# A Gram stage in a recommendation tower: one 108x108 float32 product for four neighbouring items in place of four 27x27 strip products

## What is computed

```python
e = jnp.stack([tbl_0[ids[:, 0]], ..., tbl_25[ids[:, 25]]], axis=1)      # 2048 x 26 x 128
combined = jnp.concatenate([e, r_dense_x[:, None, :]], axis=1)          # 2048 x 27 x 128
interact = jnp.einsum('bfd,bgd->bfg', combined, combined)
z = interact[:, _TRIU_I, _TRIU_J]                                       # 351 pairs
h = jnp.concatenate([z, r_dense_x], axis=1)
h = jnp.maximum(h @ W_top1 + b_top1, 0.0)                               # 479 -> 512
h = jnp.maximum(h @ W_top2 + b_top2, 0.0)                               # 512 -> 256
y = h @ W_top3
```

## Time and profile before

| | before |
|---|---|
| median of 3 runs | 605.26 us (597.03 to 606.22) |
| the profiled execution | 600.04 us, its span 598.2 us |
| mean granted TensorE clock | 0.778 of full speed |
| PE busy | 367.6 us (61% of the span) |
| PE weight loads busy | 335.5 us (56%) |
| POOL busy | 300.0 us (50%) |
| ACT busy | 180.2 us (30%) |
| DVE busy | 176.4 us (29%) |
| mean DMA rate | 81 GB/s |

### The profile page before, as it was taken

One profiled execution on the slowest core, in us unless ns is written; L12 is line 12 of the kernel. 1 busy time (PEld: TensorE's weight loads), 2 busy tenths in 40 slices (PEclk: granted clock), 3 DMA queues, 4 the chain that ended last, 5 costly groups with the idle time before them and its releaser, 6 DMA issues.

```text
span 598.2 us, 13682 instructions
## 1 busy us (share of the span) xinstructions
PE 367.6 (61%) x6108; PEld 335.5 (56%) x6108; DVE 176.4 (29%) x390; ACT 180.2 (30%) x257; POOL 300.0 (50%) x295
## 2 busy tenths in 40 slices
PE   0130836858386846867584847774685568467847
PEld 0130836848285736766483847674575467356846
DVE  3112932625031521343132411352034313102100
ACT  1140411414143332315050412334151425034401
POOL 6774584637455473636376654737373737500000
PEclk9965866869588876958596877979597779659865
DMA  5981521436131462144124423144221413111010
GB/s 114 217 222 46 113 54 46 118 72 137 36 98 45 118 90 84 49 83 115 60 71 76 106 70 90 48 104 100 73 61 46 127 35 94 41 57 59 3 57 0
DMA packets 46250, 48.40 MB, mean 81 GB/s; under 512 B 18504, under 2 KB 38801, under 8 KB 46192
## 3 DMA queue, kind: packets, MB, share of 16 engines
q1 hardware_dynamic: 36544, 28.63, 21.3%
q0 software_dynamic: 9216, 18.89, 11.7%
q10 hardware_dynamic: 432, 0.00, 0.0%
HBM read 37.01 MB, written 10.49 MB: 79 GB/s over the span
## 4 chain that ended last, share of the span: by engine, by line
PE 54%; issue 31%; ACT 4%; DVE 3%; another core or an unknown queue 3%; DMA 3%; SPq 1%; ACTq 0%; DVEq 0%
PE ps_o L559 21%; PE ps_g L587 13%; PE ps_l L611 9%; PE ps_l L622 5%; PE ps_t L574 5%; ACT emb L337 1%; PE ps_l L631 1%; DMA emb<-tbl 1%; ACT emb L330 1%; DVE tab L437 1%; DMA turn<-gram 1%; DMA zl<-turn 1%; ACT h L355 1%; DVE onehot L449 1%
## 5 line engine op out<-in xcount | busy, mean ns | idle before, releaser
L214 POOL DMA_INDIRECT rows<-tbl,idx x288 | 299.2, 1039 | 218.0 <-PE ps_t L574 137.2
L559 PE MATMUL ps_o<-onehot,tab 128*128 128x256 f32 (+1 forms) x1024 | 141.8, 299 | 31.4 <-DVE tab L437 19.4
L559 PEld LDWEIGHTS ps_o<-onehot,tab 128*128 128x128 f32 (+1 forms) x1024 | 134.9, 205 | 35.9 <-DVE tab L437 19.7
L587 PE MATMUL ps_g<-emb 128*27 128x27 f32 x4096 | 79.8, 220 | 119.0 <-issue 116.5
L449 DVE TENSOR_SCALAR onehot<-ids_b,row_of 128x512 fp32r<-128x512 int32 (+1 forms) x256 | 113.1, 495 | 92.4 <-PE ps_o L559 58.4
L587 PEld LDWEIGHTS ps_g<-emb 128*27 128x27 f32 x4096 | 63.0, 133 | 136.2 <-issue 131.6
L337 ACT COPY emb<-ps_t 128x512 f32<-128x512 f32 (+1 forms) x80 | 89.9, 1185 | 136.8 <-PE ps_t L574 136.8
L574 PE MATMUL ps_t<-ident,rows 128*128 128x128 f32 x304 | 53.6, 313 | 54.0 <-issue 39.6
L330 ACT COPY emb<-ps_o 128x512 f32<-128x512 f32 x32 | 38.2, 1193 | 131.5 <-remote 65.0
L574 PEld LDWEIGHTS ps_t<-ident,rows 128*128 128x128 f32 x304 | 39.2, 159 | 58.0 <-issue 40.9
L611 PE MATMUL ps_l<-zh,w_sb 117*128 117x256 f32 (+1 forms) x216 | 48.8, 348 | 8.6 <-DVE zl L469 8.6
(11 more groups left out here) (26 smaller groups left out, 143.7 us busy)
## 6 DMA issues: line engine op xcount, KB each, us to landing
ids_b<-ids_oh SPq DMA_DIRECT2D x32, 256.0 KB
turn<-gram SPq DMA_DIRECT2D x16, 432.0 KB
rows<-tbl,idx POOLq DMA_INDIRECT x288
turn<-gram SPq DMA_DIRECT2D x16, 208.0 KB
zl<-turn SPq DMA_DIRECT2D x64, 40.5 KB
emb<-tbl SPq DMA_DIRECT2D x8, 256.0 KB
emb<-tbl SPq DMA_DIRECT2D x8, 192.0 KB
rows<-r_dense_x SPq DMA_DIRECT2D x16, 64.0 KB
```

The costliest lines, as they stand in the source:

```text
L214: nc.gpsimd.indirect_dma_start(out=rows[u][:, v, :], out_offset=None, in_=gathered[GATHERED.index(SLOT_OF[v])], in_offset=bass.IndirectOff ...
L559: last = nc.tensor.matmul(ps_o[n % 2][:, j, :], tab[0:r, UNIT * o + j, part, k, :], onehot[m % BUFS][0:r, i, j, :], start=(k, j, part) == ...
L587: last = nc.tensor.matmul(ps_g[h][SLOT * s:SLOT * s + NF, NF * g:NF * (g + 1)], v, v, start=True, stop=True)
```

## The change

Four neighbouring items, whose 108 columns lie side by side in `emb`, are multiplied with themselves in one 108x108 product; the four 27x27 blocks on its diagonal are the wanted matrices, the other twelve are not used. A bank now holds four such products, so a tile fills eight banks in turn (`GBANKS`) instead of two, in the same two PSUM banks. The even ones are copied by DVE, the odd ones by ACT, each 108 rows by 432 elements, to the one `gram` buffer left, and PE waits before each bank for the copy of the bank two before. Both copies wait for the stores of the tile before. `spread` stores only the diagonal blocks: 27 rows at a time, two DMAs for each of the four, eight in all. The order of items inside a tile becomes s + 4g, so the copies of x and of y read or write with a stride. The zeroing of the banks goes. One-hot buffers become four of one block each, instead of three of two blocks. The `keep_gram` in the diff is ACT's; DVE has the same over `range(0, GBANKS, 2)`.

```diff
-KB = 2
+KB = 1
-BUFS = 3
+BUFS = 4
-S4, SLOT = 4, 32
+S4, SM = 4, 4
 GROUPS = TILE // S4
-HALF = GROUPS // 2
+BANKG = 4
+GBANKS = GROUPS // BANKG
+GCOLS = SM * NF
+TURN_DMAS = 2 * S4
-        gram = [sb(f"gram{u}", [P, NF, GROUPS]) for u in range(2)]
+        gram = sb("gram", [P, SM, NF, GROUPS])
+        def strip_at(s):
+            return NF * s, s % SM
+        def gram_of(h):
+            return gram[0:GCOLS].rearrange("p s j g -> p (s j) g")[:, :, BANKG * h:BANKG * (h + 1)]
+        def products_of(h):
+            return ps_g[h % 2][0:GCOLS, 0:BANKG * GCOLS].rearrange("p (g c) -> p c g", c=GCOLS)
...
             def spread(tile):
                 u = tile % 2
-                sp.wait_ge(gram_moved, 2 * tile + 2)
+                for h in range(2):
+                    sp.wait_ge(gram_kept[h], GBANKS // 2 * (tile + 1))
                 if tile >= 2:
                     sp.wait_ge(z_in[u], Z_DMAS * 16 * (tile // 2))
-                to = turn[u].ap()
-                flat = gram[u][:].rearrange("p j g -> p (j g)")
-                sp.dma_start(to[:, 0:NF * GROUPS], flat).then_inc(turn_out[u], 16)
-                sp.dma_start(to[:, NF * GROUPS:], flat[:, 0:LAST_D * GROUPS]).then_inc(turn_out[u], 16)
+                to = turn[u].ap().rearrange("(s i) n -> s i n", s=S4)
+                for s in range(S4):
+                    p, c = strip_at(s)
+                    own = gram[p:p + NF, c].rearrange("p j g -> p (j g)")
+                    sp.dma_start(to[s, :, 0:NF * GROUPS], own).then_inc(turn_out[u], 16)
+                    sp.dma_start(to[s, :, NF * GROUPS:], own[:, 0:LAST_D * GROUPS]).then_inc(turn_out[u], 16)
...
+            def keep_gram(tile):
+                if tile:
+                    act.wait_ge(turn_out[(tile - 1) % 2], TURN_DMAS * 16 * ((tile + 1) // 2))
+                for h in range(1, GBANKS, 2):
+                    act.wait_ge(gram_done, GBANKS * tile + h + 1)
+                    nc.scalar.copy(gram_of(h), products_of(h)).then_inc(gram_kept[h % 2], 1)
...
-                for h in range(2):
-                    if tile:
-                        pe.wait_ge(gram_moved, 2 * tile + h - 1)
-                    for g in range(HALF):
-                        for s in range(S4):
-                            v = item_of(t % 2, cols + GROUPS * s + HALF * h + g)
-                            last = nc.tensor.matmul(ps_g[h][SLOT * s:SLOT * s + NF, NF * g:NF * (g + 1)], v, v,
-                                                    start=True, stop=True)
+                for h in range(GBANKS):
+                    if tile or h >= 2:
+                        pe.wait_ge(gram_kept[h % 2], (GBANKS * tile + h) // 2)
+                    for g in range(BANKG):
+                        b = cols + S4 * (BANKG * h + g)
+                        v = emb[t % 2][:, b:b + SM, :].rearrange("p b f -> p (b f)")
+                        last = nc.tensor.matmul(ps_g[h % 2][0:GCOLS, GCOLS * g:GCOLS * (g + 1)], v, v,
+                                                start=True, stop=True)
                     last.then_inc(gram_done, 1)
```

67 lines of the change are left out of this document (31 added, 36 removed).

## The result

The changed kernel is slower: 614.57 us median (609.63 to 615.66, 4 runs) against 605.74 (597.03 to 607.81, 4 runs) beside it. The ratio is 1.021, with a 95% interval of 1.014 to 1.027.

What follows compares the result with a forecast made beforehand. The prediction took PE's pauses in the strip product phases, read as running out of instructions, as the bound. It summed 598.2 - 79.5 + 7.8 - 12 + 11 = 525.5 us of span, forecasting 528 us, range 500 to 570.

Steps and rivals of the forecast that it cites:

- The pauses are PE running out of instructions: Strip product phases: pauses come from instruction supply and all go with fewer instructions; fourteen long phases 188.7 to 109.2 us, -79.5 us.
- the cases in which the pauses go: Whole kernel: faster by over 2% (under 593 us) in all cases but the last two rivals; chance 0.91.
- PE is not held: Product phases: emptying a bank on ACT takes 1.8 us a cycle, as long as filling both banks; phase 7.8 us.
- +7.8: Phases of tiles 14 and 15, short before the change: they lengthen to 7.8 us each, +7.8 us together.
- 0.5 us: Start of a product phase: allowance for both copying engines still busy with layer 1's outputs or the split of z.
- Array work 0.114 us a record: 108-column products on PE: 0.114 us per record, 0.23 per product, 7.3 us for the 32 of a tile.
- the copy on ScalarE: Emptying a bank on ACT, 432 elements: taken as 0.75 us, bounds 0.52 and 1.04.
- The clock: -12 us: PE work after seven even tiles' phases: full clock after dense products saves 1.5 to 1.9 us each, -12 us.
- The z chain: +11 us: Gram stores and z loads: eight stores issue 2.3 us longer; +0.8 us at six borders, +2.0 at three last chains.
- the row of tile 5: Evidence for the z chain: stores issued at 264.08, loads at 271.79, 7.7 us, laid to other transfers on the way.
- The pauses stay: Rival on product phases: pauses belong to entering products, 9 us stay in fourteen phases, clock gain lost; 666 us, chance 0.04.
- The 662 us: Whole kernel under the skill's array-packing rule: strips at 3.3 to 4.5 us against 7.3, change costs about 64 us.

Runs made afterwards that it cites:

- e2: The kernel before with the gathers of tiles 2 to 15 left out, those tiles working on old rows; 487.95 us, ratio 0.812 to the kernel before.
- e13: The changed kernel, tiles 1 to 15 making two banks four times over, without the last six banks' handshakes; 479.89 us, ratio 1.005 to the kernel before.
- e14: The changed kernel, tiles 1 to 15 making one product per bank instead of four, all eight handshakes kept; 480.97 us, ratio 1.009 to the kernel before.
- e9: The changed kernel unaltered, run again later with no late signals; 502.48 us, ratio 1.047 to the kernel before (480.57 us).
- e10: The kernel before unaltered, run again later for a trace with all gathers and no late signals; 477.32 us.

## Why the prediction was wrong

- **"The pauses are PE running out of instructions", all gone: -79.5 us.** This step failed. The packets did fall to 24, as said, but instructions account for at most 31 of the 116.5 us of pauses. The rest was TensorE held up, or its signals late, during gathers; e2 takes 108 us off the phases with every instruction in place. In the changed kernel that came back as 9 to 11 us in five even tiles' first handshake: the phases rose from 196.6 to 213.1 us instead of falling to 125. The sentence "inferred, not shown" stood beside it, and the cases in which the pauses go still got 0.91. GpSimd's rows beside the trickle show the coincidence, the times of the instruction packets speak against the reading, and ScalarE's [10.02 <-remote] in tile 5 is a delay in telling of work that is on record as done.
- **"PE is not held" by the banks, 7.8 us a phase.** The size came out for even tiles with the signals on time (8.0 us) and for tiles 14 and 15 (8.0 and 7.7, so the **+7.8** as well), but by luck: the array work is 1 us less than costed, and TensorE is held for 1.12 us. Wrong for odd ones (11.2): "0.5 us" for engines still busy at the start of a phase was VectorE's queue of split, y copy and four one-hots, 2.7 us more.
- **Array work 0.114 us a record.** 0.0975 measured (e13); the copy on ScalarE 0.52 for 0.75. Both were put too high, the first by 1 us a tile.
- **The clock: -12 us.** Its direction is right: granted clock 0.858 for 0.778, and with signals on time the stretches from even to odd tile shrink by 10.4 us (162.7 to 152.3). e13 and e14, which differ in how dense their phases are, differ by 12.1 us there (150.1 and 162.2). In the result itself the late signals hid it (+5.2).
- **The z chain: +11 us.** Wrong in sign. Eight stores take 2.9 us to issue, as costed, but land 2.7 us after that, where two took 8.3; the row of tile 5 was one behind the id loads. The stretches from odd to even tile lost 27 us in e9 and 9 us in the result.
- **The rivals.** "The pauses stay" was nearest: its condition (more than 6 us of pause in a phase) held in five tiles, though neither for its reason nor in fourteen. In e2 2.7 us a phase are left of 7.3 (43.9 and 116.5 us over 16), one pause of some 2 us where an instruction packet moves. The Trainium skill, Runtime: NRT & Kernel Launch, section Instruction fetch mechanics, calls the cost of crossing between instruction blocks "mostly hidden". It was right to doubt the prediction's reading by it, but for strips at this pace the crossing is not hidden here: it is those 2 us. With signals on time the change costs 25 us of span (e9, e10) because 61 us more in the phases outweigh 38 us less between them; no rival had that sum. The 662 us that the prediction gives for the strips' own rate are another mechanism than this rival, to which it refers; against strips with their pauses, signals on time, that term is 18 us (e13), not 64.

## To carry to other kernels

"Issue" only says that the profile has no name for a wait. Before giving it one, look at what every other engine does in those microseconds, GpSimd's descriptor work among them, and at the two or three places where the wait is missing. A change that cuts a long run of independent work into eight waits on other engines makes TensorE depend on those engines' queues: list what stands ahead of the first copy there. See also whether the times of the instruction packets fit before blaming them. And measure a kernel whose stages hide each other by removing a stage before optimising it; phases of 85, 103 and 116 us gave the same time here.

## What the hardware showed that was not expected

- With gathers issued back to back (1.25 us apart), TensorE's signals arrived some 10 us late, and got through 1.1 to 1.9 us after the bursts shown; strips trickled. The kernel before: 599 us so, 478 to 482 us in other runs with the same gathers. Nothing here shows what makes the difference.
- With strips of 6.7 ns an instruction, a pause, mostly of 1 to 2.6 us, stands at the same record of a tile in before, e2 and e10, where an instruction packet moves.
- A strided 432-element copy from PSUM in runs of four takes ScalarE 0.52 us and VectorE 0.60 us.
- Two loads of 256 KB, issued 2.2 us ahead of two stores in the same queue, delay their landing from 2.2-3.4 us to 6.8-9.1 us, and less the further ahead they are; issued behind them, they stretch the issue of four following loads from 1.43 to 4.97 us.
